# Address table and counts wholly on VectorE; GpSimd copies all columns before one block of roots; the router one step sooner

## The chip, the cores and the metric

The kernel runs on one core of one Trainium2 chip. The core has five engines that run side by side, each through its own list of instructions in order: TensorE (PE in the profile, with PEld for its weight loads), VectorE (DVE), ScalarE (ACT), GpSimd (POOL) and SyncE (SP), which issues most DMAs. They wait for each other on semaphores. The metric is the device time of one execution in microseconds (us), the median over runs.

## The reference, cut to what matters

The program computes one transformer block on 64 sequences of 64 tokens with 256 features: a conditional mixture of experts (four experts of which each sequence takes two, and a shared one), and then a gated feed-forward layer with a layer norm, in which every second token of the flat list also goes through a router and eight small experts.

```python
out = out + w_be[:, e][:, None, None] * mask[e][None, :, None] * y        # first part, y = gelu(c @ ew1 + b) @ ew2
...
sh = _ln(jax.nn.silu(x1) * x2, s_ln_g, s_ln_b)                            # second part, all tokens
shared_out = jnp.einsum('bth,dh->btd', sh, sw3) + sb3
x_moe = x[index_b, index_t]                                               # selected tokens
expert_scores = jax.nn.sigmoid(x_moe @ eg_w.T + eg_b)
top1_idx = jnp.argmax(expert_scores + exp_bias, axis=-1)
...
final_out = shared_out.at[index_b, index_t].set(shared_moe_out + expert_moe_out)
return x + final_out
```

## The kernel before, in words

**First part.** TensorE works through chunks of tokens: 14 chunks of 256 tokens with the shared expert (`hidden_shared` and `output`, lines L1210 and L1240), then four short "lead" chunks, one for each expert, then chunks of 242 columns gathered for one expert at a time, at the end two more shared chunks. ScalarE applies the gelu (L1074), VectorE splits the result into a high and a low fp16 half (`splits`, L1442 and L1444), and TensorE's `output` of a chunk waits for all four splits of that chunk.

Which columns go into a gathered chunk is decided on the device. VectorE works out ranks and counts, TensorE turns them into a row of addresses, and VectorE writes that row to the table `tab` (L1603 to L1608, signal `at_ready`). GpSimd then makes a second row from it, `xtab` (L1858 to L1864), the place of each piece in `X`. Meanwhile VectorE runs `splits(12)`, then writes the expert numbers and chunk counts to `tab` (L1614 to L1628, signal `slots_ready`), then runs `splits(13)`. After `slots_ready` GpSimd copies nine pieces of 22 columns for lead chunk 0 and four for lead chunk 1 (L1882, signal `x_staged`). TensorE's first lead chunk waits for the first nine of them.

**Second part.** Eight steps k = 0 to 7 of 512 tokens each. The functions and lines are:

- TensorE: `first(k)` L614, `centre(k)` L627, `second(k)` L640. For the selected tokens `router` L647, `gfirst` L656 in five parts (1, 2, 2, 2 and 2 experts), `turn_hot` L663.
- ScalarE: `c_high` L505, `silu` L511, `square` L517, `g_high` L525. For the selected tokens `gsilu` L531 and `score` L537, a sigmoid. ACT_TABLE_LOAD rows are switches between sets of functions; the sigmoid stands in another set than silu.
- VectorE: `gated` L758, `c_low` L751, `g_low` L763, `rows` L778 (four instructions, scales and adds the output of `second(k)`, and so frees its two banks). For the selected tokens `ggated` L801 and L808, `choose` L815 to L823.
- GpSimd: 128 copies of one selected column each (L947, in eight groups of 16 whose addresses are loaded from a table by L942, signal `cg_pool`), and the reciprocal roots for steps 0 to 3 (`roots`, 15 small dependent instructions, L972 to L979, signal `var_taken`). The roots of steps 4 to 7 come from ScalarE and VectorE.

The order is written out by hand in each engine's loop over k; nothing is scheduled. `first(k)` needs `gated(k-1)`, `centre(k)` needs `g_low(k)`, `router` needs `cg_pool`, and `second(k)` needs that `rows(k-1)` has read the banks. The copies can begin when VectorE has added the last gathered chunk to `acc` (`summed_all`).

Of the kernel before, what the change touches and what calls it, by code (L numbers as in the profile page):

```python
# [84 lines left out]
def program(nc, a):  # L85
    with ExitStack() as ctx:
# [140 lines left out]
        at_ready = sem("at_ready")  # L227
# [144 lines left out]
        tms = stf[:, 868:868 + 2 * MG]  # L372
        qms = stf[:, 876:876 + 2 * MG]
# [124 lines left out]
        def stage2_act(act):  # L498
# [66 lines left out]
            for k in range(NQ):  # L565
# [3 lines left out]
                if k == 6:  # L569
                    gsilu(0, 0)  # L570
# [30 lines left out]
        def stage2_pe(pe, output_late):  # L601
# [143 lines left out]
        def stage2_dve(dve, link, late_store):  # L745
# [25 lines left out]
            def rows(k):  # L771
                dve.wait_ge(x_rows_in[k], 16)
                dve.wait_ge(u_done, 6 if k == 4 else k + 1)
                if k < 4:
                    dve.wait_ge(var_taken, k // 2 + 1)
# [105 lines left out]
            for k in range(NQ):  # L881
# [3 lines left out]
                if k == 6:  # L885
                    ggated(0, 0)
# [44 lines left out]
        def stage2_pool(pool, link):  # L931
# [29 lines left out]
            def roots(q):  # L961
                taken = [q * 14]
# [6 lines left out]
                pool.wait_ge(sq_ready, 2 * q + 2)  # L969
                two = slice(2 * q * MG, (2 * q + 2) * MG)  # L970
# [18 lines left out]
            def group_in_front():  # L989
# [421 lines left out]
        def _(dve):  # L1411
# [175 lines left out]
            for u in range(2):  # L1587
# [7 lines left out]
                                        ALU.subtract).then_inc(hot_ready, 1)  # L1595
            dve.wait_ge(v_hi, 1)
# [9 lines left out]
            tv = tab[:, 0:NR * ROW].rearrange("p (r k) -> p r k", k=ROW)  # L1606
            link(nc.vector.tensor_copy(lead_tab, fa[:, NR * SLOTS:NSLOT]))
            nc.vector.tensor_copy(tv[:, :, 0:SLOTS],  # L1608
                                  fa[:, 0:NR * SLOTS].rearrange("p (r j) -> p r j", j=SLOTS)).then_inc(at_ready, 1)
            splits(12, 0)  # L1610
            dve.wait_ge(at_ready, 1)
            ce = yw[0:1, 0:4 * NR].rearrange("p (k r) -> p k r", k=4)
# [340 lines left out]
```

## Time and profile before

| what | value |
|---|---|
| median of 3 runs | 555.73 us (555.04 to 556.38) |
| the profiled execution's own time | 554.09 us |
| its span (first to last instruction) | 552.1 us |
| TensorE busy | 539.6 us, 98% of the span |
| VectorE, ScalarE, GpSimd busy | 396.9, 261.9, 177.3 us |

A row of the timeline gives the start in us from the span's start, the length of the group of instructions in us, engine, line, operation, tiles and their shapes, the number of instructions (x12), and in brackets how long the engine had been idle before, and what ended it. Lengths of neighbours on one engine overlap a little, since an instruction is counted until its writes have landed; where a pitch is wanted, starts are subtracted. 1.95 us lie between the profiled execution's own time and its span.

### The profile page before, as it was taken

Reading aid. Unit: us, or ns where it says so; the run is one execution under the profiler, and the core shown is the slowest. Engines: PE = TensorE matmul, PEld = TensorE weight load, DVE = VectorE, ACT = ScalarE, POOL = GpSimd, SP = SyncE. Lnnn points to the kernel's source line nnn. Section 1 sums busy time; section 2 is a strip of 40 time slices with the busy share of each in tenths; the row PEclk is TensorE's granted clock in tenths of the full one; section 3 lists DMA queues with packets and bytes.
Section 4 is the critical chain, followed back from the end, with each engine's and each line's share of the span. In section 5 each row is a group of like instructions: output and inputs, shape, how many; then the busy total and the mean of one; then the engine's idle time right before and its main releaser. Section 6 shows DMA issues by size and latency. Waiting matters only on the chain.

```text
span 552.1 us, 16532 instructions
## 1 busy us (share of the span) xinstructions
PE 539.6 (98%) x5082; PEld 481.1 (87%) x5083; DVE 396.9 (72%) x1046; ACT 261.9 (47%) x632; POOL 177.3 (32%) x566
## 2 busy tenths in 40 slices
PE   8999999999999999999999999999999999999895
PEld 5888888886889999999999999999999999865774
DVE  5979988674975757677675684887786645767585
ACT  6665766751434444343443433434424434539470
POOL 0280000000464523535335243342242410298700
PEclk9999999999999999999999999999999999999999
DMA  7722245300100002323310000000000000192233
GB/s 262 257 113 67 86 152 152 96 2 4 37 1 3 2 2 78 116 79 119 113 78 3 2 2 1 3 2 2 3 4 3 2 5 4 47 365 80 87 121 115
DMA packets 28476, 36.88 MB, mean 67 GB/s; under 512 B 4762, under 2 KB 24115, under 8 KB 28132
## 3 DMA queue, kind: packets, MB, share of 16 engines
q1 hardware_dynamic: 28292, 35.57, 19.6%
q8 instruction: 47, 0.77, 0.6%
q14 instruction: 41, 0.34, 0.2%
q0 software_dynamic: 96, 0.20, 0.1%
HBM read 27.30 MB, written 8.53 MB: 65 GB/s over the span
## 4 chain that ended last, share of the span: by engine, by line
PE 87%; POOL 4%; issue 3%; DVE 2%; POOLq 1%; DMA 1%; SPq 1%; ACT 0%; DVEq 0%; ACTq 0%
PE ps_out L1240 41%; PE ps_hidden L1210 40%; POOL W L947 2%; PE ps_hidden L656 2%; DMA W<-in_xT 1%; PE ps_out L1289 1%; DVE hbuf L1444 1%; PE ps_turn L640 0%; POOLq L942 0%; PE ps_hidden L640 0%; SPq L1021 0%; PE ps_small L640 0%; PE ps_hidden L614 0%; DVE W L1427 0%; PE ps_out L678 0%
## 5 line engine op out<-in xcount | busy, mean ns | idle before, releaser
L1240 PE MATMUL ps_out<-hbuf,W 128*128 128x242 f16 (+4 forms) x2304 | 242.9, 266 | 0.5 <-DVE W L1427 0.5
L1240 PEld LDWEIGHTS ps_out<-hbuf,W 128*128 (+1 forms) x2304 | 218.3, 98 | 17.5 <-DVE W L1427 0.8
L1074 ACT ACTIVATE h<-ps_hidden,b 128x242 f32<-128x242 f32 (+3 forms) x384 | 151.9, 462 | 67.3 <-PE ps_hidden L1210 64.5
L1882 POOL COPY xs<-X 128x88 f16 x334 | 111.1, 381 | 174.6 <-PE ps_hidden L1210 169.4
L1210 PE MATMUL ps_hidden<-xs,W 128*128 128x242 f16 (+2 forms) x1536 | 156.1, 262 | 1.1 <-issue 1.1
L1210 PEld LDWEIGHTS ps_hidden<-xs,W 128*128 (+1 forms) x1536 | 143.3, 98 | 9.3 <-issue 1.6
L1444 DVE TENSOR_TENSOR hbuf<-h,hbuf 128x484 f16<-128x484 f32 (+4 forms) x192 | 127.5, 664 | 7.5
L1735 DVE SCALAR_TENSOR_TENSOR acc<-ytmp,wrow,acc 128x44 f32 (+1 forms) x334 | 62.9, 260 | 80.5 <-ACT ytmp L1164 69.4
L1442 DVE CAST hbuf<-h 128x484 f16<-128x484 f32 (+4 forms) x192 | 83.8, 436 | 13.9 <-ACT h L1074 12.7
L1210 PE MATMUL ps_hidden<-X,W 128*128 128x256 f16 (+1 forms) x768 | 87.1, 273 | 0.9 <-DVE W L1427 0.8
L1164 ACT ACTIVATE ytmp<-ps_out,b 128x242 f32<-128x242 f32 (+3 forms) x64 | 25.5, 450 | 124.2 <-PE ps_out L1240 124.2
L1210 PEld LDWEIGHTS ps_hidden<-X,W 128*128 128x128 f16 x768 | 74.8, 98 | 11.0 <-DVE W L1427 1.6
L947 POOL COPY W<-acc 128x2 f32 x128 | 26.8, 274 | 37.9 <-DVE f L1803 35.3
L1858 POOL CAST ytmp<-tab 1x385 f32<-1x385 int32 x1 | 0.6, 631 | 102.1 <-DVE tab L1608 102.1
L1083 ACT ACTIVATE acc<-ps_out,b 128x256 f32<-128x256 f32 x28 | 11.7, 469 | 39.8 <-PE ps_out L1240 39.8
L1093 ACT ACTIVATE W<-stage 128x1024 f16<-128x1024 f32 x16 | 17.0, 1061 | 14.5 <-DMA stage<-in_ew 14.5
L1450 DVE SCALAR_TENSOR_TENSOR W<-stage,W 128x1024 f16<-128x1024 f32 x16 | 19.2, 1220 | 5.3 <-ACT W L1093 5.2
L614 PE MATMUL ps_hidden<-W,F 128*128 128x512 f16 x96 | 22.2, 379 | 0.2 <-DVE W L751 0.2
L614 PEld LDWEIGHTS ps_hidden<-W,F 128*128 128x128 f16 x96 | 9.2, 98 | 10.0 <-DVE W L751 0.7
L511 ACT ACTIVATE W<-ps_hidden,fb 128x512 f32<-128x512 f32 x8 | 5.6, 694 | 10.6 <-PE ps_hidden L614 10.6
L1466 DVE TENSOR_REDUCE acc<-W 128x16 f32<-128x336 f32 (+1 forms) x24 | 10.3, 499 | 0.0
L517 ACT ACTIVATE W<-ps_out 128x128 f32<-128x128 f32 x32 | 8.4, 277 | 3.1 <-PE ps_out L627 2.9
(316 smaller groups left out, 298.4 us busy)
## 6 DMA issues: line engine op xcount, KB each, us to landing
stage<-in_ew SPq DMA_DIRECT2D x16, 512.0 KB, 3.9
stage<-in_xR SPq DMA_DIRECT2D x8, 512.0 KB, 3.9
moved_rows<-stage SPq DMA_DIRECT2D x8, 512.0 KB, 2.6
X<-moved_rows SPq DMA_DIRECT2D x8, 512.0 KB, 10.1
out_rows<-X SPq DMA_DIRECT2D x16, 256.0 KB, 2.2
W<-in_xT SPq DMA_DIRECT2D x7, 512.0 KB, 9.3
W<-in_fw SPq DMA_DIRECT2D x1, 2304.0 KB, 11.6
W<-in_sw SPq DMA_DIRECT2D x4, 256.0 KB, 3.6
```

The costliest lines, as they stand in the source:

```text
L614: mm = pe.matmul(ps1[which][:, :], fw(wp, which, db), chl[:, k % CR, 2 * xp + db, :], start=(n == 0), stop=(n == 5))
L947: i = nc.gpsimd.tensor_copy(cgT[:, :, at + j:at + j + 1], column(col))
L1074: i = nc.scalar.activation(h32[:, j, k * size:(k + 1) * size], ps1[j][:, k * size:(k + 1) * size], ACT.Gelu_apprx_tanh, bias=b1[:, bass.ds ...
L1093: nc.scalar.activation(W[:, bass.ds(e * WE + at, 1024)], stage[:, k % 2, :], ACT.Copy, scale=WS).then_inc(hi_ready, 1)
L1164: i = nc.scalar.activation(ytmp[:, bass.ds(parity, 1), db, 0:size].rearrange("p o c -> p (o c)"), psy2[:, bass.ds(parity, 1), db * size:(d ...
L1210: mm = pe.matmul(out, w1(e, wp, db, hb), rhs(xp, db), start=(n == 0), stop=(n == 5))
L1240: mm = pe.matmul(out, w2(e, wp, hb, db), h, start=(n == 0), stop=(n == 3 * HB - 1))
L1442: nc.vector.tensor_copy(hi, src).then_inc(h_hi, 1)
L1444: nc.vector.tensor_tensor(lo, src, hi, ALU.subtract).then_inc(h_ready, 1)
L1450: nc.vector.scalar_tensor_tensor(W[:, bass.ds(e * WE + (at + 2048), 1024)], stage[:, k % 2, :], WS, W[:, bass.ds(e * WE + at, 1024)], ALU. ...
L1735: i = nc.vector.scalar_tensor_tensor(at, y, wrow[:, bass.ds(weight + j, 1)], at, ALU.mult, ALU.add)
L1882: i = nc.gpsimd.tensor_copy(xs[:, parity, :, j * SEG:(j + 1) * SEG], X[:, :, bass.ds(cols[j], SEG)])
```

## The change

It has three parts. In the first part of the kernel VectorE writes the expert numbers and chunk counts right after it has sent `hot_ready`, ahead of `splits(11)`, and after the address row it makes `xtab` itself (five instructions of 412 elements on one partition); `slots_ready` now comes after those, ahead of `splits(12)`, and GpSimd's seven instructions for `xtab` are gone. In the second part GpSimd makes all 128 copies and then one block of 15 root instructions for steps 0 to 3 (16 columns wide where two blocks were 8 wide). The router and the first two parts of `gfirst` go behind `centre(4)` of step 5, with their silus, the sigmoid and the gating; `second(0)` to `second(3)` and `rows(0)` to `rows(3)` go later.

```diff
@@ stage2_act
                 if k + 2 < NQ:
                     c_high(k + 2)
-                if k == 6:
-                    gsilu(0, 0)
                 if k >= 1:
                     square(k - 1)
                 g_high(k)
-                if k == 6:
+                if k == 5:
+                    gsilu(0, 0)
                     gsilu(0, 1)
                     score(0)
+                if k == 6:
                     gsilu(0, 2)
                     gsilu(0, 3)
@@ stage2_pe
                 first(k)
-                if k == 6:
+                centre(k - 1)
+                if k == 5:
                     pe.wait_ge(fwr_in, 16)
                     router(0)
                     gfirst(0, 0)
                     gfirst(0, 1)
-                centre(k - 1)
-                if k >= 4:
-                    second(k - 4)
                 if k == 6:
+                    second(0)
                     gfirst(0, 2)
                     gfirst(0, 3)
+                    second(1)
                 if k == 7:
+                    second(2)
                     gfirst(0, 4)
                     turn_hot(0)
+                    second(3)
@@ stage2_dve
                 if k == 6:
-                    ggated(0, 0)
+                    choose(0)
                 g_low(k)
                 if k == 0:
                     late_store(1)
-                if k == 4:
+                if k == 5:
+                    ggated(0, 0)
+                    ggated(0, 1)
+                if k == 6:
                     rows(0)
-                if k == 5:
-                    rows(1)
-                if k == 6:
-                    ggated(0, 1)
-                    rows(2)
                     ggated(0, 2)
                     ggated(0, 3)
-                    choose(0)
+                    rows(1)
+                if k == 7:
+                    rows(2)
             rows(3)
@@ stage2_pool
-                pool.wait_ge(sq_ready, 2 * q + 2)
-                two = slice(2 * q * MG, (2 * q + 2) * MG)
+                pool.wait_ge(sq_ready, 4)
+                two = slice(0, 4 * MG)
...
                 for at in range(48, P, 16):
-                    if at == 96:
-                        roots(0)
                     i = copies(at, addresses(0, at, 0))
                 i.then_inc(cg_pool, 1)
-                roots(1)
+                roots()
                 x_rows(0)
@@ vector, between hot_ready and splits(11)
+            link(nc.vector.tensor_scalar(above, siota[0:1, 0:NR], G[0:1, 19, 1:2], None, ALU.is_ge))
+            for e in range(2, E):
+                link(nc.vector.scalar_tensor_tensor(above, siota[0:1, 0:NR], G[0:1, 19, e:e + 1], above,
+                                                    ALU.is_ge, ALU.add))
+            link(nc.vector.tensor_copy(tv[:, :, SLOTS], above))
...
+            link(nc.vector.tensor_copy(tab[:, NR * ROW:NR * ROW + 2], G[0:1, 27, 0:2]))
+            link(nc.vector.tensor_copy(tab[:, NR * ROW + 3:NR * ROW + 4], G[0:1, 27, 2:3]))
@@ vector, behind the address row
+            link(nc.vector.tensor_scalar(srow, fa, 1.0 / BS, 0.5 / BS - 0.5, ALU.mult, ALU.add))
+            link(nc.vector.tensor_scalar(srow, srow, ROUND, None, ALU.add))
+            link(nc.vector.tensor_scalar(srow, srow, -ROUND, None, ALU.add))
+            link(nc.vector.scalar_tensor_tensor(fa, srow, -2.0, fa, ALU.mult, ALU.add))
+            nc.vector.tensor_scalar(xtab[:, :], fa, float(TOK), None, ALU.min).then_inc(slots_ready, 1)
             splits(12, 0)
-            dve.wait_ge(at_ready, 1)
...
             splits(13, 1)
```

TensorE's list in steps 5 and 6 before, from `second(0)` on (L614 is `first`, L627 `centre`, L640 `second`, L647 `router`, L656 `gfirst`):

```order
L640 MATMUL ps_turn<-V,W 128x256 x6
L640 MATMUL ps_small<-V,W 128x256 x6
L614 MATMUL ps_hidden<-W,F 128x512 x12
L627 MATMUL ps_out<-stage,W 128x128 x8
L640 MATMUL ps_turn<-V,W 128x256 x6
L640 MATMUL ps_small<-V,W 128x256 x6
L614 MATMUL ps_hidden<-W,F 128x512 x12
L647 MATMUL ps_hidden<-stage,W 128x9 x2
L656 MATMUL ps_hidden<-W 128x128 x12
L627 MATMUL ps_out<-stage,W 128x128 x8
```

The same place now, from `first(5)` on; every line number of this part is one lower:

```order
L613 MATMUL ps_hidden<-W,F 128x512 x12
L626 MATMUL ps_out<-stage,W 128x128 x8
L646 MATMUL ps_hidden<-stage,W 128x9 x2
L655 MATMUL ps_hidden<-W 128x128 x12
L613 MATMUL ps_hidden<-W,F 128x512 x12
L626 MATMUL ps_out<-stage,W 128x128 x8
L639 MATMUL ps_turn<-V,W 128x256 x6
L639 MATMUL ps_small<-V,W 128x256 x6
L655 MATMUL ps_hidden<-W 128x128 x16
L639 MATMUL ps_turn<-V,W 128x256 x6
L639 MATMUL ps_small<-V,W 128x256 x6
```

Router and `gfirst` moved ahead of `first(6)`, and `second(0)` and `second(1)` behind it.

ScalarE's list in step 6 before, from `silu(6)` (L511) to `gsilu(0, 2)` (L531):

```order
L511 ACTIVATE W<-ps_hidden,fb 128x512
L531 ACTIVATE hbuf<-ps_hidden,fb 128x128
L517 ACTIVATE W,stage<-ps_out 128x128 x4
L525 ACTIVATE W<-W 128x512
L531 ACTIVATE hbuf<-ps_hidden,fb 128x128 x2
L537 ACT_TABLE_LOAD
L537 ACTIVATE stage<-stage 128x9
L531 ACT_TABLE_LOAD
L531 ACTIVATE hbuf<-ps_hidden,fb 128x128 x4
```

ScalarE's list now, from `g_high(5)` (L524) to `g_high(6)`:

```order
L524 ACTIVATE W<-W 128x512
L530 ACTIVATE hbuf<-ps_hidden,fb 128x128 x3
L536 ACT_TABLE_LOAD
L536 ACTIVATE stage<-stage 128x9
L510 ACT_TABLE_LOAD
L510 ACTIVATE W<-ps_hidden,fb 128x512
L516 ACTIVATE W,stage<-ps_out 128x128 x4
L524 ACTIVATE W<-W 128x512
```

Both table loads now stand ahead of `silu(6)`; before they stood behind `g_high(6)`.

VectorE's list now, from `gated(6)` (L759) through `choose` (L816 to L824) and `g_low(6)` (L764) to `rows(0)` (L779):

```order
L759 SCALAR_TENSOR_TENSOR W<-ps_hidden1,stage,W 128x512
L816 TENSOR_TENSOR stage<-stage 128x8
L817 TENSOR_REDUCE stage<-stage 128x1
L818 SCALAR_TENSOR_TENSOR stage<-stage 128x8
L819 TENSOR_REDUCE stage<-stage 128x1
L820 TENSOR_SCALAR stage<-stage 128x8
L822 TENSOR_TENSOR stage<-stage 128x8
L823 TENSOR_REDUCE stage<-stage 128x1
L824 TENSOR_TENSOR stage<-stage 128x1
L764 SCALAR_TENSOR_TENSOR W<-W 128x512
L779 SCALAR_TENSOR_TENSOR X<-ps_turn,stage,X 128x256 x2
L779 SCALAR_TENSOR_TENSOR X<-ps_small,stage,X 128x256 x2
```

Before, `rows(0)` stood in step 4 and `choose` at the end of step 6, behind `g_low(6)` and `rows(2)`.

## Rows read from the trace of the kernel before

**Rows 1.** The profile's head: the span.

```profile
span 552.1 us, 16532 instructions
```

**Rows 2.** Timeline of TensorE around the first lead chunk.

```profile
152.23 5.40 PE L1240 MATMUL ps_out<-hbuf,W 128*128 128x256 f16 x48
...
159.57 4.24 PE L1210 MATMUL ps_hidden<-xs,W 128*128 128x198 f16 x48 [0.88 <-issue]
```

**Rows 3.** Timeline of GpSimd, same place: pieces for lead chunks 0 and 1.

```profile
156.55 3.73 POOL L1882 COPY xs<-X 128x88 f16 x13 [5.16 <-issue]
```

**Rows 4.** Timeline of VectorE, same place.

```profile
136.47 0.42 DVE L1598 TENSOR_TENSOR V<-ps_out,V 128x256 f16<-128x256 f32 x1 [6.82 <-ACT F L1151]
...
143.71 0.54 DVE L1608 CAST tab<-ytmp 1x385 int32<-1x385 f32 x1
...
153.65 0.14 DVE L1628 CAST tab<-lease 1x1 int32<-1x1 f32 x1
```

**Rows 5.** Timeline of TensorE in the second part, steps 5 to 7.

```profile
505.32 0.82 PE L640 MATMUL ps_turn<-V,W 128*128 128x256 f16 x6
...
506.63 2.75 PE L614 MATMUL ps_hidden<-W,F 128*128 128x512 f16 x12
509.22 0.61 PE L627 MATMUL ps_out<-stage,W 128*128 128x128 f16 x8
511.28 0.83 PE L640 MATMUL ps_turn<-V,W 128*128 128x256 f16 x6 [1.45 <-DVE X L778]
...
516.37 0.58 PE L647 MATMUL ps_hidden<-stage,W 128*128 128x9 f32 x4 [1.01 <-POOL W L947]
516.81 2.92 PE L656 MATMUL ps_hidden<-W 128*128 128x128 f32 x24
...
521.32 3.90 PE L656 MATMUL ps_hidden<-W 128*128 128x128 f32 x32
...
527.65 0.61 PE L627 MATMUL ps_out<-stage,W 128*128 128x128 f16 x8
...
529.41 1.95 PE L656 MATMUL ps_hidden<-W 128*128 128x128 f32 x16
```

**Rows 6.** Timeline of GpSimd: one instruction of each block of roots, the last 32 copies.

```profile
502.72 1.19 POOL L973 TENSOR_SCALAR stage<-stage 128x8 int32<-128x8 int32 x1
...
510.69 5.54 POOL L947 COPY W<-acc 128x2 f32 x32 [1.27 <-issue]
...
516.58 0.20 POOL L973 TENSOR_SCALAR stage<-stage 128x8 int32<-128x8 int32 x1
```

**Rows 7.** Timeline of GpSimd, cut to the first nine of those 32 copies.

```profile
510.69 1.16 POOL L947 COPY W<-acc 128x2 f32 x9 [1.27 <-issue]
```

**Rows 8.** Timeline of VectorE in the second part.

```profile
502.63 1.22 DVE L751 TENSOR_TENSOR W<-acc,W 128x1024 f16<-128x1024 f32 x1
504.11 0.69 DVE L763 SCALAR_TENSOR_TENSOR W<-W 128x512 f16<-128x512 f32 x1 [0.27 <-ACT W L525]
...
526.94 0.15 DVE L815 TENSOR_TENSOR stage<-stage 128x8 f32<-128x8 f32 x1
...
528.55 0.75 DVE L758 SCALAR_TENSOR_TENSOR W<-ps_hidden,stage,W 128x512 f32<-128x512 f32 x1
...
530.61 0.87 DVE L778 SCALAR_TENSOR_TENSOR X<-ps_turn,stage,X 128x256 f32<-128x256 f32 x2
```

**Rows 9.** Timeline of ScalarE around the sigmoid.

```profile
521.75 0.64 ACT L531 ACTIVATE hbuf<-ps_hidden,fb 128x128 f32<-128x128 f32 x2
522.42 1.28 ACT L537 ACT_TABLE_LOAD   x1
523.71 0.21 ACT L537 ACTIVATE stage<-stage 128x9 f32<-128x9 f32 x1
523.94 1.28 ACT L531 ACT_TABLE_LOAD   x1
...
526.56 0.69 ACT L511 ACTIVATE W<-ps_hidden,fb 128x512 f32<-128x512 f32 x1 [0.18 <-PE ps_hidden L614]
```

More of the change, by code:

```diff
@@ L959, in gather, with roots @@
                 i.then_inc(cg_pool, 1)
-            def roots(q):
-                taken = [q * 14]
+            def roots():
+                taken = [0]
                 def link(i):
@@ L1595, in _ @@
                                         ALU.subtract).then_inc(hot_ready, 1)
+            tv = tab[:, 0:NR * ROW].rearrange("p (r k) -> p r k", k=ROW)
+            above, evens = yw[0:1, 414:414 + NR], yw[0:1, 450:450 + (NR + 1) // 2]
+            link(nc.vector.tensor_scalar(above, siota[0:1, 0:NR], G[0:1, 19, 1:2], None, ALU.is_ge))
[3 more added lines that the diff above has]
+            link(nc.vector.tensor_copy(tv[:, :, SLOTS], above))
+            total, even = G[0:1, 27, 0:1], G[0:1, 27, 1:2]
+            link(nc.vector.tensor_tensor(total, G[0:1, 19, E - 1:E], G[0:1, 18, E - 1:E], ALU.add))
+            link(nc.vector.tensor_scalar(evens, siota[0:1, 0:NR:2], total, None, ALU.is_lt))
+            link(nc.vector.tensor_reduce(even, evens, AX.X, ALU.add))
+            link(nc.vector.tensor_scalar(even, even, -2.0, 1.0, ALU.mult, ALU.add))
+            link(nc.vector.tensor_tensor(even, even, total, ALU.add))
+            link(nc.vector.tensor_scalar(total, total, -2.0, None, ALU.add))
+            link(nc.vector.tensor_scalar(G[0:1, 27, 2:3], even, -1.0, 1.0, ALU.mult, ALU.add))
+            link(nc.vector.tensor_copy(tab[:, NR * ROW:NR * ROW + 2], G[0:1, 27, 0:2]))
+            link(nc.vector.tensor_copy(tab[:, NR * ROW + 3:NR * ROW + 4], G[0:1, 27, 2:3]))
             dve.wait_ge(v_hi, 1)
@@ L1613, in _ @@
-            for e in range(1, E):
-                link(nc.vector.tensor_scalar(ce[:, e, :], siota[0:1, 0:NR], G[0:1, 19, e:e + 1], None, ALU.is_ge))
-            link(nc.vector.tensor_tensor(ce[:, 1, :], ce[:, 1, :], ce[:, 2, :], ALU.add))
-            link(nc.vector.tensor_tensor(ce[:, 1, :], ce[:, 1, :], ce[:, 3, :], ALU.add))
-            link(nc.vector.tensor_copy(tv[:, :, SLOTS], ce[:, 1, :]))
-            total, even = G[0:1, 27, 0:1], G[0:1, 27, 1:2]
-            link(nc.vector.tensor_tensor(total, G[0:1, 19, E - 1:E], G[0:1, 18, E - 1:E], ALU.add))
@@ L1621, in _ @@
-            link(nc.vector.tensor_scalar(ce[:, 0, 0:(NR + 1) // 2], siota[0:1, 0:NR:2], total, None, ALU.is_lt))
-            link(nc.vector.tensor_reduce(even, ce[:, 0, 0:(NR + 1) // 2], AX.X, ALU.add))
-            link(nc.vector.tensor_scalar(even, even, -2.0, 1.0, ALU.mult, ALU.add))
-            link(nc.vector.tensor_tensor(even, even, total, ALU.add))
-            link(nc.vector.tensor_scalar(total, total, -2.0, None, ALU.add))
-            link(nc.vector.tensor_scalar(G[0:1, 27, 2:3], even, -1.0, 1.0, ALU.mult, ALU.add))
@@ L1627, in _ @@
-            link(nc.vector.tensor_copy(tab[:, NR * ROW:NR * ROW + 2], G[0:1, 27, 0:2]))
-            nc.vector.tensor_copy(tab[:, NR * ROW + 3:NR * ROW + 4], G[0:1, 27, 2:3]).then_inc(slots_ready, 1)
+            link(nc.vector.tensor_copy(tv[:, :, 0:SLOTS],
+                                       fa[:, 0:NR * SLOTS].rearrange("p (r j) -> p r j", j=SLOTS)))
+            link(nc.vector.tensor_scalar(srow, fa, 1.0 / BS, 0.5 / BS - 0.5, ALU.mult, ALU.add))
+            link(nc.vector.tensor_scalar(srow, srow, ROUND, None, ALU.add))
@@ L1854, in _ @@
             nc.gpsimd.memset(tab[:, :], 0).then_inc(const_ready, 1)
-            pool.wait_ge(at_ready, 1)
-            at = tab[:, 0:NR * ROW].rearrange("p (r k) -> p r k", k=ROW)[:, :, 0:SLOTS]
-            row, whole = srow, xtab[:, :].bitcast(F32)
-            link(nc.gpsimd.tensor_copy(row[:, 0:NR * SLOTS].rearrange("p (r j) -> p r j", j=SLOTS), at))
-            link(nc.gpsimd.tensor_copy(row[:, NR * SLOTS:NSLOT], lead_tab))
-            link(nc.gpsimd.tensor_scalar(whole, row, 1.0 / BS, 0.5 / BS - 0.5, ALU.mult, ALU.add))
-            link(nc.gpsimd.tensor_scalar(whole, whole, ROUND, None, ALU.add))
-            link(nc.gpsimd.tensor_scalar(whole, whole, -ROUND, -2.0, ALU.add, ALU.mult))
-            link(nc.gpsimd.tensor_tensor(whole, whole, row, ALU.add))
-            link(nc.gpsimd.tensor_scalar(xtab[:, :], whole, float(TOK), None, ALU.min))
             pool.wait_ge(slots_ready, 1)
```

11 lines of the change are left out of this document (3 added, 8 removed).

## The prediction

> **What bounds the kernel now.** I read the timeline of TensorE first, from end to end, since its matmuls fill nearly the whole span of 552.1 us [rows 1]. A change to another engine is then worth what it takes from TensorE's waits, or adds to them, unless TensorE stops being the engine that ends last. So the question is where TensorE stands idle near the three edits. Before the first lead chunk it stands 0.88 us [rows 2]. In the second part it stands before `second(1)`, put down to `rows(0)`, and before `router`, put down to the copies [rows 5]. Then I read GpSimd, VectorE and ScalarE at the same places, to see what made these waits end.
>
> For sums I use pitches, start to start. One `first` takes 506.63 to 509.22, 2.59 us, and one `second` 505.32 to 506.63, 1.31 us [rows 5]. A `centre` takes 0.45 us (0.61 less the 0.16 that rows overlap), `router` 0.44, the first two parts of `gfirst` 2.8, parts three and four 3.75, part five 1.8 (each the row's length less that overlap). Then the wait before `second(1)` is 511.28 - 509.22 - 0.45 = 1.6 us, and that before `router` 516.37 - 511.28 - 1.31 - 2.59 = 1.2 us. Together 2.8 us.
>
> **Edit 1, the table.** The first lead chunk waits for nine pieces that GpSimd starts at 156.55 [rows 3], 2.8 us after VectorE's last table instruction ended at 153.79 [rows 4]. TensorE goes on at 159.57, so the nine take 2.9 us more. Now the counts, some 3.5 us of small instructions, stand in the 6.82 us in which VectorE waits before L1598 [rows 4]: cost nothing; if that cover were gone, `splits(11)` would start 3.5 us late. The row for `xtab` is five instructions of 412 elements behind L1608, which ends at 144.25. The nearest row is L1608 itself, 0.54 us for 385 elements [rows 4]. Upper bound five times 0.6, lower bound five times the 0.14 of the one-element instruction L1628; they are long, so I take 2.6. So `slots_ready` comes at 146.9 and not at 153.8, and the nine pieces are there at 152.6, six us ahead of TensorE. The 0.88 us go. What is late instead is `splits(12)`, queued behind the five instructions: it starts 2.6 us later, at 146.9. Before, it ran from 144.2 to the counts, 3.5 us ahead of 153.8: 6.0 us, in which GpSimd's seven table instructions ran beside it. Without these I take 4.5 us, an estimate; 6.0 is the upper bound. It ends at about 151.4, and the `output` that needs it starts at 152.23 [rows 2]. That leaves 0.8 us; at the upper bound it would be 0.7 us late. Term: **-0.9 us**.
>
> **Edit 2, the copies without the roots between them.** The first block of roots is slow: L973 takes 1.19 us there and 0.20 us in the second block [rows 6]. It began at 502.72, 0.09 us after L751 of VectorE, which ran 1.22 us, and ended 0.06 us after it [rows 8]. So GpSimd stands still while VectorE runs L751 (and L763, 0.69 us). The Trainium skill states this in "SBUF — State Buffer", section "SBUF: two separate sides": the two engines share a port pair as an exclusive lock, held for a whole instruction, and the loser blocks fully. By that rule the trace agrees, and the copies meet the same lock as the roots.
>
> The 96th copy is done at 502.4, just ahead of the roots. The last 32 now follow at once. A copy takes 0.12 us start to start ((1.16 - 0.20) / 8, [rows 7]). Without any hold 32 would take 3.9 us plus address loads. But a step of the main loop without other work is `first` and `centre`, 3.1 us, and in each VectorE runs one L751 and one L763, 1.9 us together. That leaves 1.2 us, ten copies, and about two more that are caught under way: 12 per 3.1 us. So 32 take 8.1 us and `cg_pool` comes at 510.5. Bounds: 6.7 us, if the last copy gets by ahead of the third L751, near 508.9, and 9.0 us, if the copies also run into the third L763, near 510.4. I take 8.1, the middle one, since the rate is made of whole steps.
>
> **Edit 3, the router in step 5.** With `second(0)` gone from step 4, `first(5)` starts at 505.32 where `second(0)` did, and `centre(4)` ends at 505.32 + 2.59 + 0.05 + 0.45 = 508.4. The router's wait ends at 510.5 + 0.15 = 510.65: a wait of 2.25 us, where 1.6 + 1.2 stood before. What is queued behind it: `first(6)` and all of steps 6 and 7.
>
> Then the sigmoid. Its two table loads stood where ScalarE had slack; now they stand ahead of `silu(6)`, and `gated(6)`, `choose`, `g_low(6)` and `rows(0)` follow it on VectorE, and `second(1)` waits for `rows(0)`. From the start of `router`: router and gfirst 3.2, handover 0.2, two silus 0.6, load 1.28, sigmoid 0.23, load 1.28, `silu(6)` 0.7 [rows 9], `gated` 0.7, `choose` 1.6 (526.94 to 528.55), `g_low` 0.65, `rows(0)` four times 0.4, handover 0.1 [rows 8]: 12.15 us. TensorE gets to `second(1)` after 3.2 + 2.59 + 0.45 + 1.31 + 3.75 = 11.3 us. Wait 0.9 us. In step 7 `rows` starts 530.61 - 527.65 = 2.95 us after the start of `centre(6)` [rows 5, 8]; `rows(2)` ends 1.65 later, at 4.6, and TensorE is at `second(3)` after 0.45 + 1.31 + 1.8 + 0.1 = 3.7: wait 0.9 to 1.0. `second(4)` waits for `rows(3)`, 0.25 + 1.6 against 0.45 + 1.31: 0.1 to 0.2. Together 2.0 us.
>
> A rule that would make this worse: "ScalarE: Activation LUTs", section "What ACT_TABLE_LOAD costs", of the Trainium skill counts 1283 ns for the load and some 1380 ns of drain for each switch. The trace shows no drain behind the load: 522.42 + 1.28 is 523.70 and the sigmoid starts at 523.71 [rows 9].
>
> Hidden: the roots are now one block of 4.2 us (15 at 0.28) to at most 7 us from 510.5, read by `rows(0)` only near 521; if that cover were gone each us would be one of `second(1)`'s wait. The gather of token rows, issued behind them, comes some 4 us sooner than before. The stores that SyncE issues after each `rows` move back in steps 0 to 2, and end as before from step 4 on. All matmuls are the same in number, so behind `second(4)` the tail shifts as a whole.
>
> **Sum.** Waits after: 2.25 + 2.0 = 4.25, before 2.8: +1.45. Table -0.9. Together **+0.6 us** (0.55 rounded up). The profiled execution took 554.09 us, 1.95 more than its span, so it becomes 554.7. It stands 1.64 us under the median of the runs shown, 555.73; there the same difference gives **556.3 us**. A measurement of this kernel tells a difference from none at about 0.2%, 1.1 us.
>
> **The rivals.**
> - *The last copy gets by ahead of the third L751.* The router's wait is then 2.25 - 1.4 = 0.85 us: +0.6 - 1.4 gives 554.9. Three copies more by 508.9 decide it (0.4 us). For it: my rate could be 5% off. Chance 0.15.
> - *Faster.* ScalarE and VectorE keep up, so `second(1)` and `second(3)` wait for nothing. It needs `rows(0)` 0.9 us sooner than the chain of rows adds up to, and `rows(2)` as well. +0.6 - 2.0 = -1.4: 554.3; with the first rival on top 552.9. Against it: each link is a row. Chance 0.1.
> - *The copies are held longer,* up to 9.0 us or a little over: +0.9, 557.2. For it: three whole pairs of L751 and L763 fall into the stretch. Chance 0.18.
> - *The table brings nothing*, because `splits(12)` then takes its 6.0 us or more and ends 0.7 to 0.9 us after 152.23, and `output` waits there for what the lead chunk no longer waits: +0.9, 557.2. For it: GpSimd's pieces now run beside it and take the same lock. Chance 0.1.
> - *A switch costs 2.66 us.* `silu(6)` is then two times 1.38 later, and `second(1)` with it: 559.1. Its page is the one on ScalarE named above. Chance 0.02.
>
> **Numbers.** The forecast, 555.5 to 557.1 by itself, has 0.45. Faster by over 1.1 us: the second rival and a third of the first, and a little noise, 0.17. Slower by over 1.1 us: most of the third and fourth, the fifth, and the upper end of the forecast, 0.33. Range: 554.5 leaves out most of the second rival, 557.7 holds the third and fourth.
>
> **What would show it.** Right: no wait before the first lead chunk and none before the `output` ahead of it; L1882's first row some 7 us sooner; a `router` wait of 2 us or more put down to L947; waits before `second(1)` and `second(3)` put down to L778, near 0.9 each; copies with lengths over 0.6 us wherever L751 or L763 of the changed kernel runs. Wrong: a `router` wait under 1.2 us, or `second` without waits, or a new wait at `output` before the lead chunks.

## The result, and the profile after

| | changed kernel | kernel before |
|---|---|---|
| median of 22 runs each, side by side | 556.38 us (554.24 to 558.3) | 555.09 us (553.45 to 556.8) |
| ratio, 95% interval | 1.0026 (1.0015 to 1.0036) | |
| profiled execution, span | 555.5 us | 552.1 us [rows 1] |
| mean granted clock in it | 0.995 | 0.999 |

The changed kernel is 1.3 us slower by the medians; the forecast said 0.6 us. A second comparison gave 1.0009 (0.9992 to 1.0027) for the same code, which by itself holds no change. So the change costs some 0.1 to 0.3%. Four executions in the comparisons below fell into a slower state (566.5, 946, 1148 and 1458 us) and are left out of every number here.

TensorE's timeline after, to be laid beside [rows 2] and [rows 5]:

```profile
159.83 4.25 PE L1209 MATMUL ps_hidden<-xs,W 128*128 128x198 f16 x48
...
505.55 2.75 PE L613 MATMUL ps_hidden<-W,F 128*128 128x512 f16 x12
...
510.72 0.58 PE L646 MATMUL ps_hidden<-stage,W 128*128 128x9 f32 x4 [1.90 <-POOL W L948]
511.16 4.55 PE L655 MATMUL ps_hidden<-W 128*128 128x128 f32 x24
...
519.89 3.74 PE L655 MATMUL ps_hidden<-W 128*128 128x128 f32 x32
524.49 0.83 PE L639 MATMUL ps_turn<-V,W 128*128 128x256 f16 x6 [0.87 <-DVE X L779]
...
533.06 0.83 PE L639 MATMUL ps_turn<-V,W 128*128 128x256 f16 x6 [0.84 <-DVE X L779]
```

The first lead chunk, at 159.83, has no bracket any more. In the second part there is a bracket at the router and one each at `second(1)` and `second(3)`, as forecast. The row at 511.16 is the surprise: the same 24 matmuls took 2.92 us before [rows 5] and take 4.55 now. Stretches of the changed kernel round that row (busy us and count of instructions of each engine, then the granted clock of TensorE, and what the DMAs did):

```profile
509.00:511.00 2.00, 0.28 (x3) 0.31 (x3) 1.73 (x3) 1.52 (x9) 1.91 (x6) 1.00 0.00 0
...
512.00:515.00 3.00, 3.00 (x16) 3.00 (x15) 0.42 (x2) 0.37 (x1) 2.17 (x11) 0.50 0.00 0
...
516.00:518.00 2.00, 2.00 (x11) 0.94 (x10) 0.61 (x2) 1.95 (x5) 0.88 (x1) 1.00 0.22 49
```

TensorE stands still for 1.9 us, starts again, and from 512 to 515 us its clock is at 0.50, the lower level of 1.2 GHz, though it is busy all the time. Work that waits for nothing takes longer there: 4.55 - 2.92 = 1.63 us.

GpSimd's timeline after:

```profile
150.37 6.63 POOL L1873 COPY xs<-X 128x88 f16 x13 [110.19 <-issue]
...
495.60 14.97 POOL L948 COPY W<-acc 128x2 f32 x64 [1.21 <-issue]
```

VectorE's timeline after, the table and the first two of `rows(0)`:

```profile
133.34 0.14 DVE L1611 CAST tab<-lease 1x1 int32<-1x1 f32 x1
137.71 0.43 DVE L1614 TENSOR_TENSOR V<-ps_out,V 128x256 f16<-128x256 f32 x1 [4.22 <-ACT F L1150]
...
145.52 0.36 DVE L1625 TENSOR_SCALAR ytmp<-ytmp 1x412 f32<-1x412 f32 x1
...
147.32 0.36 DVE L1629 TENSOR_SCALAR xtab<-ytmp 1x412 int32<-1x412 f32 x1
147.61 0.41 DVE L1441 CAST hbuf<-h 128x512 f16<-128x512 f32 x1
...
522.78 0.87 DVE L779 SCALAR_TENSOR_TENSOR X<-ps_turn,stage,X 128x256 f32<-128x256 f32 x2
```

The counts end at 133.48, and VectorE still idles 4.22 us behind them, so they cost nothing. The five `xtab` instructions take 2.1 us, and the pieces of the first lead chunks start at 150.37, 6.2 us sooner than in [rows 3]. The copies of the second part end at 495.60 + 14.97 = 510.57. `rows(0)` starts at 522.78, behind the whole chain of sigmoid and `choose`. ScalarE's timeline round the sigmoid:

```profile
516.39 1.28 ACT L536 ACT_TABLE_LOAD   x1
517.68 0.21 ACT L536 ACTIVATE stage<-stage 128x9 f32<-128x9 f32 x1
517.91 1.28 ACT L510 ACT_TABLE_LOAD   x1
519.21 0.69 ACT L510 ACTIVATE W<-ps_hidden,fb 128x512 f32<-128x512 f32 x1
```

Both loads now stand ahead of `silu(6)` (L510), and nothing lies between a load's end and the next ACTIVATE.

### The profile page after: what moved, and what is told of

It reads as the page before. It is cut to its first block and busy times, and to the rows that moved or that the text cites. A ratio compares the mean times of both kernels' runs of the same rounds, so it can differ in the third digit from the quotient of the medians.

```text
span 555.5 us, 16512 instructions
## 1 busy us (share of the span) xinstructions
PE 542.4 (98%) x5082; PEld 482.6 (87%) x5083; DVE 396.1 (71%) x1049; ACT 262.0 (47%) x632; POOL 171.2 (31%) x544
## 5 line engine op out<-in xcount | busy, mean ns | idle before, releaser
L1873 POOL COPY xs<-X 128x88 f16 x334 | 116.5, 398 | 277.5 <-PE ps_hidden L1209 167.3
L948 POOL COPY W<-acc 128x2 f32 x128 | 29.2, 289 | 36.7 <-DVE f L1804 35.4
L759 DVE SCALAR_TENSOR_TENSOR W<-ps_hidden,stage,W 128x512 f32<-128x512 f32 x8 | 6.0, 751 | 7.0 <-ACT W L510 3.8
L510 ACT ACTIVATE W<-ps_hidden,fb 128x512 f32<-128x512 f32 x8 | 5.6, 696 | 11.0 <-PE ps_hidden L613 10.9
```

Of the source, the lines that this page charges most:

```text
L948: i = nc.gpsimd.tensor_copy(cgT[:, :, at + j:at + j + 1], column(col))
L1873: i = nc.gpsimd.tensor_copy(xs[:, parity, :, j * SEG:(j + 1) * SEG], X[:, :, bass.ds(cols[j], SEG)])
```

## What the mean clock of each execution tells

Each timed execution comes with its mean granted clock. A "fall" here is a stretch of some 3 to 4 us at 0.50 before the last matmul. Behind its last matmul TensorE idles, and the trace has it at the lower level there in every kernel; that is not counted. The fourteen profiles of this document show what the mean stands for. The nine without a fall have 0.997 to 0.999, the four with one fall 0.994 to 0.996. The last one, "Roots ahead of the last 32 copies", has one stretch of some 14 us at 0.50 and a mean of 0.986. I read 0.989 to 0.993 as two falls; no profile caught such an execution. Sorted that way, the executions of the kernel before from all the comparisons below:

| the kernel before, beside | no fall | one fall |
|---|---|---|
| the first four experiments | 19 at 554.39 us | 9 at 555.98 us |
| the next four | 16 at 554.52 us | 8 at 555.84 us |
| the next three | 12 at 554.41 us | 11 at 556.13 us |
| the last one | 12 at 554.24 us | 5 at 556.23 us |

(means of each group.) By these means a fall costs 1.3 to 2.0 us, and the kernel before has 33 in 92 executions, 0.36 each, and never two in one. The changed kernel has, in its 30 executions of two comparisons, 8 with none, 18 with one and 4 with two: 26 falls, 0.87 each. I use this sorting in what follows, since it takes the scatter of the clock out of small differences. What it leaves is not small: executions of one kernel without a fall differ by 0.2 to 0.5 us (standard deviation), so a mean of four is good to about 0.2 us.

## Experiments

**The table alone.** Only edit 1, with the second part as before (cut, against the kernel before):

```diff
+            link(nc.vector.tensor_scalar(above, siota[0:1, 0:NR], G[0:1, 19, 1:2], None, ALU.is_ge))
...
+            nc.vector.tensor_scalar(xtab[:, :], fa, float(TOK), None, ALU.min).then_inc(slots_ready, 1)
             splits(12, 0)
-            dve.wait_ge(at_ready, 1)
```

> Only edit 1 is made: VectorE makes the counts and the address table, and the second part stands as in the kernel before. By the forecast's sum the wait of 0.88 us ahead of the first lead chunk goes and nothing takes its place: 0.9 us under the kernel before, ratio 0.9984. Rival, the table brings nothing since the start of splits(12) is put off or since the start of the span differs anyway from run to run: ratio 1.000.

Median 554.68 us, ratio 0.9993 (0.9979 to 1.0007): by itself undecided. Sorted by clock: four executions without a fall at 553.56 against 554.39 us, eight with one at 554.96 against 555.98: 0.8 and 1.0 us less, which is the forecast's 0.9. The median hid it, since 8 of 12 executions had a fall where 9 of 28 had in the kernel before; whether that is chance these numbers don't tell. It matters below, since the waits of this kernel in the second part are those of the kernel before.

**The second part alone.** Edits 2 and 3, with the table as before (cut, against the changed kernel):

```diff
-            nc.vector.tensor_scalar(xtab[:, :], fa, float(TOK), None, ALU.min).then_inc(slots_ready, 1)
             splits(12, 0)
+            dve.wait_ge(at_ready, 1)
```

> Only edits 2 and 3 are made: the copies in one go, the roots in one block, the router in step 5; the table stands as in the kernel before. By the forecast's sum, waits alone, +1.45 us: ratio 1.0026. With the fall of the granted clock behind the router's wait as well, which the changed kernel's profile shows (1.6 us more for the same 24 matmuls) and which 18 of its 22 executions seem to have, +1.45 + 0.8 x 1.6 = +2.7 us: ratio 1.005. If the clock is an accident of single executions, the first number stands.

Median 556.94 us, ratio 1.0031 (1.0019 to 1.0044). Without a fall 555.85 against 554.39 us (+1.46), with one 557.15 against 555.98 (+1.17). Of the four without a fall three stand near 555.5 and one at 556.87, so +1.46 is no sharp number. TensorE's timeline of this kernel:

```profile
509.86 0.58 PE L647 MATMUL ps_hidden<-stage,W 128*128 128x9 f32 x4 [0.49 <-POOL W L949]
510.30 2.92 PE L656 MATMUL ps_hidden<-W 128*128 128x128 f32 x24
...
539.32 2.17 PE L678 MATMUL ps_out<-onesm,h 128*128 128x1 f32 x18
...
541.87 2.30 PE L695 MATMUL ps_hidden<-w3e,hbuf 128*128 128x256 f32 x6
```

Two things here were new. The router waited 0.49 us only. GpSimd's timeline says why:

```profile
495.53 3.04 POOL L949 COPY W<-acc 128x2 f32 x16 [0.90 <-issue]
498.74 10.97 POOL L949 COPY W<-acc 128x2 f32 x48 [0.18 <-issue]
```

and VectorE's, that the third `c_low` behind the 96th copy started at 509.62:

```profile
509.62 1.22 DVE L753 TENSOR_TENSOR W<-acc,W 128x1024 f16<-128x1024 f32 x1
```

The last copy ended at 509.71. That is the forecast's first rival, the last copy that gets by ahead of the third `c_low`: 1.4 us less wait. It was most likely a matter of luck. An address load stood for 0.90 us where the changed kernel's took 1.21, and TensorE was 0.5 us later than there. The kernel before, which has the same first part, has 1.20 us at that load, so the edit doesn't explain it.

And the clock fell at another place. Its stretches:

```profile
508.00:512.00 4.00, 3.51 (x31) 2.81 (x30) 3.39 (x6) 3.44 (x12) 3.66 (x15) 1.00 0.01 4
...
542.00:543.00 1.00, 1.00 (x5) 0.86 (x4) 0.90 (x4) 0.00 (x0) 0.00 (x0) 0.67 0.43 140
543.00:545.00 2.00, 2.00 (x8) 1.27 (x8) 1.29 (x4) 0.00 (x0) 0.00 (x0) 0.50 0.31 104
```

It fell behind `gvariance`, 18 matmuls of one column in 2.17 us, in which TensorE counts as busy.

**Filler ahead of the router.**

```diff
                     pe.wait_ge(fwr_in, 16)
+                    for n in range(8):
+                        pe.matmul(ps1[3][:, :], fw(0, 0, 0), chl[:, k % CR, 0, :], start=True, stop=True)
                     router(0)
```

> The changed kernel with eight more matmuls (128x128 by 128x512, into the free bank of the third and fourth hidden products, results unused, about 0.21 us each, 1.7 us in all) ahead of the router, so that TensorE works through most of the 1.9 us for which it stood. If the wait itself makes the clock fall: granted clock 1.00 all through, the 24 matmuls of the first gfirst parts take 2.9 us and not 4.55, the other waits unchanged, and the time is 1.3 to 1.6 us under the changed kernel (ratio to the kernel before near 0.9995). Rival, the fall has another cause (the matmuls on 4-byte numbers that follow, or the time since the start): clock 0.5 behind the router again, ratio 1.0026 as before.

Its timeline of TensorE (L706 is the filler):

```profile
507.92 1.89 PE L706 MATMUL ps_hidden<-W,F 128*128 128x512 f16 x8
510.03 0.61 PE L646 MATMUL ps_hidden<-stage,W 128*128 128x9 f32 x4 [0.22 <-POOL W L950]
510.50 2.92 PE L655 MATMUL ps_hidden<-W 128*128 128x128 f32 x24
```

The router starts as late as before, but TensorE works in 1.7 us of the wait, and the 24 matmuls take 2.92 us in this execution. Median 554.9 us, ratio 1.0007 (0.9992 to 1.0021). It has seven executions without a fall and five with one, 0.42 falls each: near the kernel before's share and not the changed kernel's 0.87. Those without a fall stand at 554.51 us against 554.39, +0.1, so the useless work costs nothing. That it takes the added falls away is likely from the counts, but 5 of 12 executions with a fall beside 22 of 30 can still be chance; the medians of different comparisons (1.0007 here, 1.0026 and 1.0009 for the changed kernel) can't tell by themselves.

**Router behind first(6).**

```diff
                 first(k)
-                centre(k - 1)
-                if k == 5:
+                if k == 6:
                     pe.wait_ge(fwr_in, 16)
                     router(0)
                     gfirst(0, 0)
                     gfirst(0, 1)
+                centre(k - 1)
```

ScalarE has `gsilu(0, 0)` ahead of `square(5)`, and `gsilu(0, 1)` and `score(0)` behind `g_high(6)`. VectorE's order in step 6 is `ggated(0, 0)`, `g_low(6)`, `ggated(0, 1)`, `rows(0)`, `choose(0)`, `ggated(0, 2)`, `rows(1)`, `ggated(0, 3)`, and in step 7 `rows(2)`, `g_low(7)`.

> Edits 1 and 2 stay; the router goes back behind first(6), where the copies are done already, the sigmoid and choose go back behind silu(6), second(0) to second(3) stay where the changed kernel has them, and rows(2) stands ahead of g_low(7). By the forecast's reasons: no wait at the router, none over 0.4 us at second(1) to second(3), no fall of the clock: 2.1 us less than the kernel before in the second part and 0.9 less by the table, ratio 0.9946. Rival, the step of the router is not what costs, since the longer chain behind it (gsilu, ggated, rows) then stops TensorE elsewhere: a wait of 1 us or more before the third or fourth part of gfirst or before second(1), ratio 0.998 to 1.000.

```profile
511.09 0.51 PE L646 MATMUL ps_hidden<-stage,W 128*128 128x9 f32 x4
511.45 2.92 PE L655 MATMUL ps_hidden<-W 128*128 128x128 f32 x24
...
518.16 2.05 PE L655 MATMUL ps_hidden<-W 128*128 128x128 f32 x16 [0.24 <-DVE hbuf L809]
```

Above is TensorE's timeline: no bracket at the router nor at any `second`, one of 0.24 us at the fourth part of `gfirst`. Median 550.9 us over six executions, ratio 0.9927 (0.9907 to 0.9948): 3.8 us under the kernel before, 0.8 more than expected. One execution of six had a fall, which gives 0.3 us of that. The trace has no term for the rest: the second part is 2.16 us shorter (the table under "Why the prediction was right and wrong") and the lead chunk's wait of 0.88 us is gone, 3.04 us together, the 3.0 expected. So the rest is likely scatter of six executions.

**The last 32 columns in one copy.**

```diff
-                for at in range(48, P, 16):
-                    i = copies(at, addresses(0, at, 0))
-                i.then_inc(cg_pool, 1)
+                for at in range(48, 96, 16):
+                    copies(at, addresses(0, at, 0))
+                nc.gpsimd.tensor_copy(cgT[:, :, 96:P], acc[:, :, 96:P]).then_inc(cg_pool, 1)
```

> The changed kernel, but the last 32 columns are copied by one instruction as they lie, and not as the address table selects them, so the last 32 tokens' router inputs are other ones: the part leaves out 31 of the 32 one-column copies. Forecast's reasons: GpSimd is done near 503 and the router's wait of 1.9 us goes as a whole; the clock has no wait to fall behind there; the waits before second(1) and second(3), 0.9 each, stay, since their chain starts at the router. 1.9 + 0.8 x 1.6 = 3.2 us under the changed kernel, ratio to the kernel before 0.997. Rival, TensorE's wait is only handed on to second(1): under 1 us gained, ratio 1.001.

In the timeline the router and what follows it wait for nothing, and `second(1)` waits as it did:

```profile
507.60 0.56 PE L646 MATMUL ps_hidden<-stage,W 128*128 128x9 f32 x4
...
519.73 0.83 PE L639 MATMUL ps_turn<-V,W 128*128 128x256 f16 x6 [0.87 <-DVE X L779]
...
539.80 2.77 PE L694 MATMUL ps_hidden<-w3e,hbuf 128*128 128x256 f32 x6
```

This profile is of the one execution in five with a fall, and it stands behind `gvariance` again: the row at 539.80 takes 2.77 us, 1.46 us in the kernel before.

Median 552.74 us, ratio 0.9959 (0.9944 to 0.9975). Four executions without a fall, 552.61 us against the kernel before's 554.52: -1.9; the changed kernel stood at +0.2 by the same sorting (554.65 against 554.41, in the second comparison). The 1.9 us of the router's wait go as a whole, and nothing takes their place at `second(1)`. So the last 32 copies are what the router waits for.

**Roots ahead of the last 32 copies.**

```diff
                 for at in range(48, P, 16):
+                    if at == 96:
+                        roots()
                     i = copies(at, addresses(0, at, 0))
                 i.then_inc(cg_pool, 1)
-                roots()
```

> The changed kernel with edit 2 undone in one respect: the block of roots stands ahead of the last 32 copies, as the first block did in the kernel before, while the router stays in step 5. The roots then take 4.2 to 7 us and the copies 5.5 to 8, so the copies are done at 514 to 517 and the router waits 6 to 9 us instead of 1.9: 4 to 7 us slower than the changed kernel. Rival, roots and copies are not what the router waits for: no change.

Median 566.74 us of two, ratio 1.0213 (1.0189 to 1.0236), some 10 us over the changed kernel: far more than the 4 to 7 us expected. GpSimd's timeline shows what I had left out:

```profile
505.87 0.28 POOL L973 TENSOR_SCALAR stage<-stage 128x16 f32<-128x16 f32 x1 [4.38 <-ACT W L516]
...
516.78 2.01 POOL L948 COPY W<-acc 128x2 f32 x16 [1.23 <-issue]
```

One block for four steps must wait for `square(3)` (L516), and GpSimd stands 4.38 us ahead of it with 32 copies queued behind. TensorE's timeline, and the stretch behind it:

```profile
518.94 1.00 PE L646 MATMUL ps_hidden<-stage,W 128*128 128x9 f32 x4 [11.23 <-POOL W L948]
519.79 5.43 PE L655 MATMUL ps_hidden<-W 128*128 128x128 f32 x24
```

```profile
520.00:525.00 5.00, 5.00 (x24) 4.99 (x25) 0.43 (x2) 0.37 (x1) 0.51 (x1) 0.50 0.10 26
```

The router's wait is 9.3 us longer and `gfirst` 0.9 us. The trace also gives a copy's price where VectorE is idle: 16 in 2.01 us, 0.126 each, near the 0.12 that the forecast took from [rows 7], and none lasts over 0.22 us. In the changed kernel 64 copies and their address loads took 14.97 us with VectorE at work beside them; half of these copies last 0.18 us or less, and the longest 1.24 us, as long as VectorE's `c_low` (1.22 us). By these lengths a copy that meets `c_low` is held for the whole of it. The reason that the forecast gave is a port which the two engines share and which one of them holds for a whole instruction (the Trainium skill, "SBUF — State Buffer", section "SBUF: two separate sides"); this trace agrees with it.

**second(0) ahead of the router.**

```diff
                     pe.wait_ge(fwr_in, 16)
+                    second(0)
                     router(0)
...
                 if k == 6:
-                    second(0)
```

> The changed kernel with second(0) ahead of the router in step 5 instead of in step 6. The same work, only the waits are parted otherwise: 1.3 us less at the router (0.6 left), 1.3 us more before second(1) (2.2). If only waits count and the clock falls somewhere anyway, the time stays that of the changed kernel, ratio 1.0026. If the fall needs one long wait, it now comes behind second(1) instead of behind the router and the time is again the same, with the clock at half there. If the fall is tied to the router's place, it is gone and the time is 1.3 us less.

```profile
508.91 0.61 PE L646 MATMUL ps_hidden<-stage,W 128*128 128x9 f32 x4 [0.62 <-POOL W L948]
...
521.09 0.83 PE L639 MATMUL ps_turn<-V,W 128*128 128x256 f16 x6 [2.13 <-DVE X L779]
```

The waits in the timeline are parted as expected, with the same sum (0.62 + 2.13 beside 1.90 + 0.87 us). Ratio 1.0021 (1.0005 to 1.0036), and ten falls in ten executions. Its profile caught an execution without one, so it doesn't show where they now stand; that they follow the longest wait is likely, not shown.

**Filler in the kernel before.**

```diff
+                if k == 5:
+                    for n in range(6):
+                        pe.matmul(ps1[3][:, :], fw(0, 0, 0), chl[:, k % CR, 0, :], start=True, stop=True)
                 if k >= 4:
                     second(k - 4)
```

> The kernel before with six more matmuls (128x128 by 128x512, results unused, 1.3 us in all) ahead of second(1), where TensorE stands 1.45 us. Nine of 28 executions of the kernel before show a mean granted clock of 0.994 or 0.995 and are 1.6 us longer than the 19 with 0.997 to 0.999. If that is the same fall behind the wait before second(1), hardly any execution shows 0.995 now, and the median is 0.2 to 0.5 us lower, ratio 0.9993. Rival, those falls stand elsewhere, in the first microseconds for one: the share of 0.995 stays near a third, ratio 1.000.

Ratio 1.0002 (0.999 to 1.0013). The wait before `second(1)` shrank from 1.45 to 0.15 us, and four of eleven executions still had a fall. So there is no sign that the kernel before's falls come from that wait: the rival stands.

**gvariance parted by useful work.** In the kernel before:

```diff
-            gvariance(0)
-            gsecond(0, 0, 4)
+            gvariance(0, 0, 5)
+            gsecond(0, 0, 1)
+            gvariance(0, 5, NJ)
+            gsecond(0, 1, 4)
```

> The kernel before with one matmul pair of gsecond (256 columns) moved between the 5th and 6th of the nine pairs of one-column matmuls of gvariance, so that these no longer stand in one row of 2.2 us; the same work in all. In two profiles (the order alone, the short copies) the clock stands at half for some 3.4 us right behind gvariance, at 542 and at 539 us, and 17 of 52 executions of the kernel before show a mean clock near 0.995. If the row of one-column matmuls is what lets it fall there, few or no executions show it now: median 0.3 to 0.5 us less, ratio 0.9993. Rival, half a microsecond of columns between changes nothing: the share stays near a third, ratio 1.000.

Median 554.34 against 554.89 us, ratio 0.999 (0.9977 to 1.0003). Two falls in 12 executions, beside 11 in 23 of the kernel before on that chip. That, and the two profiles above with a fall right behind `gvariance`, point to it as the place of the kernel before's falls. No profile of the kernel before caught one, and with 12 executions it isn't proved.

**The best version.** On top of the router behind `first(6)`, with `gvariance` parted as above:

```diff
                     gfirst(0, 0)
+                    second(0)
                     gfirst(0, 1)
...
-                    second(0)
```

On ScalarE `square(5)` goes behind `gsilu(0, 1)`.

> The kernel of the router behind first(6), with second(0) between the first two parts of gfirst (it fills 0.24 us in which TensorE waited for ggated ahead of part four) and with gvariance parted as in the run beside it. 0.2 us less than that kernel by the wait, up to 0.5 less where the clock no longer falls: ratio to the kernel before 0.991 to 0.993. Rival, the moved second(0) puts off the sigmoid and choose and a wait comes back before second(2) or second(3): ratio 0.995.

Median 550.56 us of six, ratio 0.9932 (0.9911 to 0.9952); in the profile, span 547.9 us, no wait of TensorE over 0.2 us is left in the second part:

```profile
509.34 0.51 PE L647 MATMUL ps_hidden<-stage,W 128*128 128x9 f32 x4
```

In this timeline the router has no bracket, and neither has `gfirst`. By the times it can't be told from the simpler version at 0.9927; by the traces its second part is 0.4 us shorter. Both beat the kernel before and the changed one.

**The changed kernel once more**, with no edit.

> The changed kernel once more, for a second profile. Two things vary from one execution to another: the copies may get by ahead of the third c_low, as in the run of the order alone (router's wait 0.49 us there, 1.90 us in the changed kernel's profile), and the clock may fall behind the router. If both were fixed, this profile shows 1.9 us and half clock behind it again. If the pass is luck, the wait is either near 1.9 or near 0.5 us, and with 0.5 the clock stays at 1.00 there.

```profile
509.92 0.58 PE L646 MATMUL ps_hidden<-stage,W 128*128 128x9 f32 x4 [2.02 <-POOL W L948]
510.36 2.92 PE L655 MATMUL ps_hidden<-W 128*128 128x128 f32 x24
```

The timeline has the same wait as the first profile, and no fall behind it: the 24 matmuls take 2.92 us. So a fall behind this wait is likely, not certain.

**rows(2) ahead of g_low(7).**

```diff
-                g_low(k)
+                if k < NQ - 1:
+                    g_low(k)
...
                 if k == 7:
                     rows(2)
+                    g_low(k)
```

> The changed kernel with rows(2) ahead of g_low(7) on VectorE in step 7, so that second(3), which waits for rows(2), no longer waits for g_low(7) as well. By the forecast's sum the 0.85 us before second(3) are a term of their own and go as a whole (g_low(7), 0.7 us later, still ends before centre(7) wants it): 0.9 us less than the changed kernel, ratio to the kernel before 1.0000 (1.0010 on the chip of the second look at the changed kernel would become 0.9993). Rival, the wait only moves to centre(7) behind it, or to second(4): 0 to 0.3 us gained.

```profile
509.94 0.58 PE L646 MATMUL ps_hidden<-stage,W 128*128 128x9 f32 x4 [1.91 <-POOL W L950]
510.38 4.55 PE L655 MATMUL ps_hidden<-W 128*128 128x128 f32 x24
...
531.35 0.83 PE L639 MATMUL ps_turn<-V,W 128*128 128x256 f16 x6
```

In the timeline `second(3)`, at 531.35, has no bracket, and neither have `centre(7)` and `second(4)` behind it. Ratio 1.0016 (0.9996 to 1.0036), by itself undecided; there were twelve falls in eleven executions. Without a fall: 554.08 against 554.24 us, -0.2, where the changed kernel stood at +0.2. That is a gain of 0.4 us of the 0.9 expected, but from means of four executions. The traces settle it: without the half clock the second part is 0.94 us shorter than in the changed kernel's first profile (34.14 against 35.08 us, in the table below), the 0.9 expected. The profile shows the rest of the mechanism again, a wait of 1.91 us and the 24 matmuls at 4.55.

## Why the prediction was right and wrong

**A finer measure than the times.** From the start of `centre(3)` to the start of `gvariance` all these kernels do the same work of TensorE, but for the filler. In the kernel before:

```profile
504.86 0.62 PE L627 MATMUL ps_out<-stage,W 128*128 128x128 f16 x8
...
538.49 2.17 PE L678 MATMUL ps_out<-onesm,h 128*128 128x1 f32 x18
```

In the changed kernel:

```profile
505.09 0.62 PE L626 MATMUL ps_out<-stage,W 128*128 128x128 f16 x8
...
541.80 2.17 PE L677 MATMUL ps_out<-onesm,h 128*128 128x1 f32 x18
```

That is 33.63 and 36.71 us. The same stretch in other profiles, one execution each, with the 1.63 us taken off where the 24 matmuls of `gfirst` took 4.55 and not 2.92 us:

| kernel | us | without the half clock | against the kernel before |
|---|---|---|---|
| before; the table alone | 33.63; 33.63 | | 0 |
| changed | 36.71 | 35.08 | +1.45 |
| changed, once more | 35.21 | | +1.58 |
| filler ahead of the router | 35.15 | | +1.52 |
| `second(0)` ahead of the router | 35.16 | | +1.53 |
| second part alone (the copies got by) | 33.68 | | +0.05 |
| last 32 columns in one copy | 32.99 | | -0.64 |
| `rows(2)` ahead of `g_low(7)` | 35.77 | 34.14 | +0.51 |
| router behind `first(6)` | 31.47 | | -2.16 |
| the best version | 31.04 | | -2.59 |

**Edit 1** was right: the wait of 0.88 us is gone from the timeline in every kernel with the edit, and the sorted times give 0.8 to 1.0 us. `splits(12)` starts at 147.61 (146.9 forecast) and takes 4.3 us (4.5).

**Edit 2** was right: the copies end at 510.57 (510.5), from the rate of twelve per step. The rate isn't safe, though: with the copies 1.4 us sooner the first rival came true in one profile of six with this order of copies and router.

**Edit 3** was right in its waits. By the forecast's own pitches they are now 510.72 - 505.55 - 2.59 - 0.45 = 2.13 us at the router (2.25), 524.49 - 519.89 - 3.75 = 0.85 at `second(1)` (0.9), and 0.84 idle at `second(3)` (0.9 to 1.0). The whole stretch is 1.45 us longer without the half clock, and the sum of waits said +1.45. The sorted times of the second part alone, +1.46 and +1.17 us, agree too, but loosely: in its one profile the copies got by and the stretch is only 0.05 us longer.

**What failed** is a step that isn't there: the sum holds waits only, and the same matmuls were taken to last as long behind a wait as before. "All matmuls are the same in number, so behind `second(4)` the tail shifts as a whole" is true of the number, not of the durations. In the changed kernel's profile the sum gives +1.45 - 0.88 = +0.57 us, and the half clock behind the router adds 1.63. Over many executions, falls went from 0.36 to 0.87 each, at 1.6 us: +0.8 us, so 1.4 in all, beside 1.3 measured in one comparison and 0.5 in the other (0.0009 of 555). The sorted times of the second comparison put the change at equal clock at 0.2 us (554.65 against 554.41); a mean of four can hardly tell that from 0.6. The forecast time, 556.3, met 556.38 in part by luck, since the kernel before ran at 555.09 in that comparison and not at 555.73.

How many of the added falls come from the router's wait is not settled. For the wait: two profiles show the half clock right behind it; executions with two falls occur only in kernels with a wait of about 2 us in the second part (the changed one, `second(0)` first, `rows(2)` first) and never in 92 of the kernel before. Against it: the table alone, without that wait, had 8 falls in 12 executions, 0.67 each, and the second part alone, with it, no more than that.

**The rivals.** The first came true in one profile, as said. "Faster" fell: the waits of 0.87 and 0.84 us are there. The rival "copies held longer" named a difference, +1.5 us, near the measured +1.3, but for another reason: the copies ended when the forecast said. "The table brings nothing" fell. "A switch costs 2.66 us" fell: 516.39 + 1.28 = 517.67, and the sigmoid starts at 517.68. Of the signs, the router's wait "of 2 us or more" was met only by the pitch (2.13) and not by the bracket (1.90), and GpSimd's pieces came 6.2 us sooner where some 7 were named.

**Open:** what decides in one execution whether the clock falls, and whether the eight falls in twelve executions of the table alone mean anything.

## What to carry to other kernels

A wait of TensorE can cost more than its length: here 1.9 us of standing had half clock behind it in two of three profiles of such a wait, worth another 1.6 us each time, and the changed kernel had a fall more in about every second execution. Keep such a term beside a sum of waits. If the wait can't go, work put into it costs nothing and may keep the clock up. Move a stage no further ahead than its last input allows: one `first` later the same router waited for nothing, and that kernel, with `second` and `rows` still in their later places, came out 0.7% faster than the one that it started from. And when differences are near 0.2%, sort the executions by their mean granted clock before comparing, or compare one stretch with the same work in two traces: here its length repeated within 0.15 us, while `centre(3)` started anywhere between 503.18 and 506.07 us.

## What was not expected of the hardware

- The granted clock fell to 0.50 behind a wait of 1.90 us and one of 1.91 us, but not behind one of 2.02 us in the same code; the 24 matmuls of 128x128 by 128 took 4.55, 4.55 and 2.92 us. Behind one of 2.13 us at another place, in the kernel with `second(0)` first, it did not fall either.
- It fell too while TensorE was busy the whole time, behind 18 matmuls of one column in 2.17 us: six matmuls of 256 columns then took 2.30 us in one profile and 2.77 us in another, and not the 1.46 us of the kernel before.
- An address load of 16 registers on GpSimd stood for 1.21 us in one execution and for 0.90 us in another at the same place, which helps decide whether 32 copies pass ahead of a `c_low`.
